# Output biases and column means of a cross-attention kernel by one product with a constant tile, under a new order of all engines

## What is computed

```
n_L0 = bv @ Wo          n_L1 = bv'_a @ Wo_a + bv'_v @ Wo_v   (bv' = ln2_b @ Wv + bv)
n_L3 = bv @ Wo          n_fc = ln_b @ fc_W
```

## Time and profile before

| | |
|---|---|
| three runs | 555.61, 556.83, 557.13 us |
| profiled execution, first to last instruction (span) | 557.1 us |
| busy: TensorE, VectorE, ScalarE, GpSimd | 98%, 86%, 80%, 86% of the span |
| mean granted clock of TensorE | 0.998 |
| transfers | 76.58 MB, mean 137 GB/s |

### The profile page before, as it was taken

The page is one execution under the profiler, slowest core; times in us unless marked ns, Lnnn a source line. Parts: engine busy times, 40 slices in busy tenths (PEclk is TensorE's granted clock), DMA queues, the critical chain, the costliest instruction groups (busy, mean ns, idle before and its releaser), DMA issues.

```text
span 557.1 us, 16210 instructions
## 1 busy us (share of the span) xinstructions
PE 545.8 (98%) x4492; PEld 534.9 (96%) x4492; DVE 478.4 (86%) x1472; ACT 447.2 (80%) x1568; POOL 480.7 (86%) x672
## 2 busy tenths in 40 slices
PE   8999999999999999999999999999999999999995
PEld 7999999999999999989999999999999999999994
DVE  2588799888999889989897997999898987998884
ACT  2799987889778797869879798877888979798663
POOL 4999997999988989979997899977999998766793
PEclk9999999999999999999999999999999999999999
DMA  8993472344553345453247263453433432221112
GB/s 238 352 326 126 118 215 90 121 147 149 172 168 111 113 143 152 149 174 124 80 139 202 67 190 102 145 172 122 139 122 115 124 105 78 77 96 58 39 40 95
DMA packets 74440, 76.58 MB, mean 137 GB/s; under 512 B 7664, under 2 KB 58224, under 8 KB 74352
## 3 DMA queue, kind: packets, MB, share of 16 engines
q1 hardware_dynamic: 74352, 75.55, 43.0%
HBM read 50.87 MB, written 24.64 MB: 136 GB/s over the span
## 4 chain that ended last, share of the span: by engine, by line
PE 87%; POOL 4%; DMA 3%; issue 2%; DVE 2%; SPq 1%; ACT 1%; DVEq 0%; POOLq 0%; ACTq 0%
PE bank L793 15%; PE bank L806 10%; PE bank L800 9%; PE bank L776 7%; PE bank L817 5%; PE bank L819 5%; PE bank L818 5%; PE bank L949 5%; PE bank L927 5%; PE bank L784 5%; PE bank L830 4%; PE bank L902 3%; PE bank L903 3%; PE bank L904 3%; DMA side_in<-in_side 1%
## 5 line engine op out<-in xcount | busy, mean ns | idle before, releaser
L1065 ACT ACTIVATE prob_L<-bank,neg_max_L 128x128 f32<-128x128 f32 x320 | 114.5, 375 | 15.7 <-DVE neg_max_L L1376 13.6
L1065 ACT ACTIVATION_READ_ACCUMULATOR prob_L<-bank,neg_max_L 128x1 f32 x320 | 68.3, 214 | 0.0
L1376 DVE TENSOR_REDUCE neg_max_L<-bank 128x2 f32<-128x256 f32 (+1 forms) x128 | 60.5, 479 | 7.1 <-PE bank L800 4.3
L1546 POOL TENSOR_TENSOR rstd_ln<-var_eps_ln,minus_half 128x2 f32<-128x2 f32 x64 | 45.2, 707 | 18.5 <-ACT var_eps_ln L1078 18.2
L994 ACT ACTIVATE oT_hi_L<-bank 128x256 fp32r<-128x256 f32 (+1 forms) x96 | 44.4, 471 | 12.4 <-PE bank L806 11.1
L1219 DVE TENSOR_TENSOR oT_lo_L<-bank,oT_hi_L 128x256 fp32r<-128x256 f32 (+1 forms) x96 | 47.2, 501 | 5.6 <-ACT oT_hi_L L994 4.9
L994 ACT ACTIVATE probT_L<-bank 128x256 f32<-128x256 f32 (+1 forms) x96 | 44.4, 470 | 9.0 <-PE bank L784 8.6
L1333 DVE BATCH_NORM_STATS2 stats_ln<-x 128x6 f32<-128x256 f32 x128 | 47.5, 413 | 0.2
L1219 DVE TENSOR_TENSOR xT_lo_L<-bank,xT_hi_L 128x512 fp32r<-128x512 f32 x64 | 43.1, 677 | 3.7 <-ACT xT_hi_L L994 3.5
L1611 POOL TENSOR_TENSOR x_bias<-x,bias_fc 128x512 f32<-128x512 f32 x32 | 41.1, 1285 | 5.8 <-DVE x L1409 5.8
L1588 POOL TENSOR_TENSOR xT_lo_L<-x_in,xT_hi_L 128x512 fp32r<-128x512 f32 x32 | 41.2, 1286 | 5.4 <-ACT xT_hi_L L994 5.4
(11 more groups left out here) (228 smaller groups left out, 2294.2 us busy)
## 6 DMA issues: line engine op xcount, KB each, us to landing
x_in<-in_x SPq DMA_DIRECT2D x32, 512.0 KB, 3.8
ctx_in<-in_ctx SPq DMA_DIRECT2D x32, 256.0 KB, 2.8
keys_out<-keys_turned SPq DMA_DIRECT2D x32, 256.0 KB, 2.2
keysT<-keys_out SPq DMA_DIRECT2D x128, 64.0 KB, 2.0
out<-y SPq DMA_DIRECT2D x32, 256.0 KB, 2.3
x_out<-x_turned SPq DMA_DIRECT2D x30, 256.0 KB, 2.2
x3T<-x_out SPq DMA_DIRECT2D x120, 64.0 KB, 2.3
side_in<-in_side SPq DMA_DIRECT2D x32, 128.0 KB, 2.7
```

The costliest lines, as they stand in the source:

```text
L1065: last = activation(at(prob[k], g)[:, b, :], block(bank, b), ACT.Exp, bias=at(neg_max[k], g)[:, b:b + 1], accum_out=at(total[k], g)[:, b:b ...
L1376: dve.tensor_reduce(at(neg_max[k], g)[:], scores, AX.X, ALU.max, negate=True).then_inc(done[f"max_{k}"], 1)
L1546: pool.tensor_tensor(at(rstd[k], g)[:], at(var_eps[k], g)[:], minus_half[:, 0:n], ALU.pow).then_inc(done[f"rstd_{k}"], 1)
```

## The change

The weighting moves from TensorE to VectorE. For an output bias, VectorE multiplies each row of the weight by its bias (the bias lies along the partitions, one column per half) and adds the halves: a `tensor_scalar`, then a `scalar_tensor_tensor` with both tensors in SBUF. For L1, L1v's two halves are added onto L1a's result. One product with `mean_of_D` then sums over the partitions, and `bias_plus` multiplies by 256 as it adds the row. For the column means VectorE adds the two halves first (`fc_added`, `M1_added`). `replicated` and its buffers are gone, and n_fc uses `output_bias` too. `load_vo_L3` waits for `weighted_L0` in place of `n_L0`. All other steps are as before.

```
@@ load_vo_L3 @@
                 prepared(sp, "N_L0")
-                prepared(sp, "n_L0")
+                prepared(sp, "weighted_L0")
...
@@ mean_M @@
-                    prepared(pe, f"M1_{a}")
+                    prepared(pe, f"M1_added_{a}")
                     bank = bank_for(pe, f"mean_M_{a}")
-                    for t in range(T):
-                        last = mm(bank[:, 0:P], mean_of_D[:], M1[a][:, t, :], start=t == 0, stop=t == T - 1)
-                    last.then_inc(done[f"mean_M_{a}"], 1)
+                    mm(bank[:, 0:P], mean_of_D[:], M1_added[a][:], start=True, stop=True).then_inc(done[f"mean_M_{a}"], 1)
...
-            def output_bias(key, attentions):
+            def output_bias(key, last_of):
+
                 def of():
+                    prepared(pe, "first_constant")
+                    prepared(pe, f"weighted_{last_of}")
                     bank = bank_for(pe, f"n_{key}")
-                    terms = []
-                    for a in attentions:
-                        prepared(pe, f"rep_{a}")
-                        pe.wait_ge(weights[f"{a}_vo"], TWO)
-                        terms += [(rep[a]["bv"][:, h, :], stage[a]["Wo"][:, h, :]) for h in range(T)]
-                    for n, (stationary, moving) in enumerate(terms):
-                        last = mm(bank[:, 0:D], stationary, moving, start=n == 0, stop=n == len(terms) - 1)
-                    last.then_inc(done[f"n_{key}"], 1)
+                    mm(bank[:, 0:D], mean_of_D[:], weighted[last_of][:], start=True, stop=True).then_inc(done[f"n_{key}"], 1)
                 return of
...
             def mean_fc():
-                prepared(pe, "gained_fc")
+                prepared(pe, "fc_added")
                 bank = bank_for(pe, "mean_fc")
-                for t in range(T):
-                    last = mm(bank[:, 0:D], mean_of_D[:], fc_gained[:, t, :], start=t == 0, stop=t == T - 1)
-                last.then_inc(done["mean_fc"], 1)
+                mm(bank[:, 0:D], mean_of_D[:], fc_added[:], start=True, stop=True).then_inc(done["mean_fc"], 1)
...
             def bias_plus(key, to, use, added):
-                dve.tensor_tensor(to[:], bank_of(use)[:, 0:D], added[:], ALU.add).then_inc(done[key], 1)
+                dve.scalar_tensor_tensor(out=to[:], in0=bank_of(use)[:, 0:D], scalar=float(D), in1=added[:],
+                                         op0=ALU.mult, op1=ALU.add).then_inc(done[key], 1)
...
+            def weighted_of(a):
+                def of():
+                    if a in LN_KEYS:
+                        prepared(dve, f"bvp_{a}")
+                        biases = [bvp[a][:, t, :] for t in range(T)]
+                    else:
+                        dve.wait_ge(weights["cols"], ONE)
+                        biases = [col("fc_b" if a == "fc" else f"{a}_bv", t) for t in range(T)]
...
+                    w = fcW if a == "fc" else stage[a]["Wo"]
+                    to = weighted[a]
+                    if a == "L3":
+                        prepared(dve, "n_L0")
+                    if a == "L1v":
+                        prepared(dve, "weighted_L1a")
+                        terms = range(T)
+                    else:
+                        before = smalls(1)
+                        dve.tensor_scalar(to[:], w[:, 0, :], biases[0], None, ALU.mult).then_inc(done["small"], 1)
+                        dve.wait_ge(done["small"], before + 1)
+                        terms = range(1, T)
+                    for t in terms:
+                        last = dve.scalar_tensor_tensor(out=to[:], in0=w[:, t, :], scalar=biases[t], in1=to[:],
+                                                        op0=ALU.mult, op1=ALU.add)
...
+            def M1_added_of(a):
+                    dve.tensor_tensor(M1_added[a][:], M1[a][:, 0, :], M1[a][:, 1, :], ALU.add).then_inc(done[f"M1_added_{a}"], 1)
...
+            def fc_added_of():
+                dve.tensor_tensor(fc_added[:], fc_gained[:, 0, :], fc_gained[:, 1, :], ALU.add).then_inc(done["fc_added"], 1)
...
-            def replicated(a):
...
-                    for t in range(T):
-                        of_bias = bvp[a][:, t, :] if a in LN_KEYS else col("fc_b" if a == "fc" else f"{a}_bv", t)
-                        last = pool.tensor_copy(rep[a]["bv"][:, t, :], of_bias.to_broadcast([P, P]))
```

More of the change, by code:

```diff
@@ L211 @@
-    "fetch_keys": [3843, 4466, 4975, 5800, 7201, 7659, 8977, 11642, 13747, 14340, 15211, 16940, 19159, 21191, 22040, 23608,
[11 rows of a table removed]
-}
-PREPARATIONS = {"run_up": 164, "M_L2": 534, "k_L2": 709, "N_L0": 1000, "n_L0": 912, "M_L0": 1364, "M_L1v": 1452, "m_L0": 1541, "m_L1v":
[14 rows of a table removed]
+    "load_x": [734, 1162, 1571, 2106, 2553, 2685, 3273, 4536, 5373, 6625, 7257, 9987, 11847, 11891, 12714, 16481, 17782, 19524, 19711,
[5 rows of a table added]
+    "load_ctx": [267, 1615, 1893, 2245, 2289, 2377, 2465, 2509, 2597, 2641, 9761, 11224, 12129, 14515, 15492, 18284, 20017, 21058, 22614,
[3 rows of a table added]
@@ new lines @@
+    "x_bias": [1589, 1714, 2112, 3012, 4160, 4408, 5846, 6197, 9605, 11605, 11729, 12582, 16015, 17153, 18238, 19450, 21290, 23407,
+        23967, 25608, 28368, 29872, 31709, 32162, 33287, 35031, 37666, 38725, 42421, 42669, 43881, 45634],
+    "stats_keys": [779, 2193, 2774, 3153, 4147, 4665, 5399, 6660, 7395, 8472, 10308, 13228, 14087, 15396, 15993, 18626, 21144, 22298,
+        23378, 24570, 27193, 28411, 29866, 30945, 33762, 35416, 36288, 37876, 39975, 41137, 43794, 44937],
+    "rstd_keys": [1016, 2775, 3523, 4670, 5137, 5361, 6321, 7014, 8404, 9954, 13249, 14935, 15159, 15780, 18761, 22629, 22894, 22993,
[15 rows of a table added]
@@ L245 @@
     "k_L2": [1],
-    "N_L0": [3],
-    "n_L0": [2],
-    "B2": [4, 7, 2, 5, 6, 0, 1, 3, 6, 7, 5, 5, 4, 7, 1, 3, 3, 3, 1, 7, 7, 4, 3, 4, 6, 3, 7, 7, 5, 3, 5, 4],
-    "M_L0": [5],
-    "M_L1v": [6],
-    "m_L0": [7],
-    "Q_L0": [0, 4, 3, 0, 6, 4, 0, 1, 5, 1, 1, 6, 0, 0, 5, 6, 6, 7, 7, 6, 5, 6, 2, 2, 0, 3, 3, 0, 0, 0, 3, 6],
-    "m_L1v": [1],
-    "S_L0": [5, 6, 5, 0, 1, 3, 1, 5, 3, 5, 5, 6, 6, 1, 0, 7, 4, 0, 3, 2, 3, 3, 1, 6, 3, 3, 3, 7, 5, 4, 4, 3],
-    "n_fc": [4],
+    "N_L0": [4],
+    "n_L0": [3],
+    "B2": [6, 2, 4, 7, 2, 6, 2, 2, 1, 7, 4, 1, 0, 4, 2, 2, 6, 5, 4, 1, 2, 7, 5, 1, 1, 4, 0, 6, 3, 2, 4, 4],
+    "M_L0": [2],
+    "M_L1v": [7],
+    "m_L0": [5],
+    "Q_L0": [1, 5, 4, 4, 1, 7, 6, 1, 3, 2, 0, 0, 4, 1, 3, 4, 6, 2, 2, 2, 0, 4, 5, 2, 2, 1, 5, 5, 1, 6, 5, 7],
+    "m_L1v": [2],
+    "S_L0": [5, 5, 2, 0, 1, 1, 1, 1, 2, 3, 4, 6, 3, 4, 2, 7, 7, 4, 5, 6, 1, 4, 1, 0, 2, 1, 7, 7, 4, 6, 4, 5],
+    "n_fc": [0],
     "mean_fc": [7],
[2 rows of a table removed]
[2 rows of a table added]
     "mean_M_L1v": [3],
[18 rows of a table removed]
-    "T_fc": [1, 5, 6, 5, 6, 6, 5, 1, 5, 6, 7, 3, 7, 4, 2, 7, 1, 5, 4, 5, 3, 3, 6, 2, 1, 3, 6, 5, 7, 7, 1, 5],
-    "OUT_fc": [1, 5, 6, 5, 5, 5, 0, 1, 5, 6, 1, 7, 7, 6, 4, 0, 2, 2, 0, 6, 2, 4, 3, 2, 1, 3, 6, 7, 3, 7, 3, 0],
[10 rows of a table removed]
[18 rows of a table added]
+    "T_fc": [1, 3, 3, 3, 4, 7, 2, 3, 2, 0, 5, 0, 4, 5, 2, 6, 0, 5, 1, 3, 2, 2, 0, 5, 4, 2, 7, 4, 2, 4, 5, 1],
+    "OUT_fc": [1, 1, 2, 3, 3, 7, 3, 3, 4, 6, 2, 0, 4, 7, 0, 5, 0, 3, 6, 3, 7, 6, 0, 4, 4, 6, 7, 4, 2, 6, 4, 6],
[9 rows of a table added]
 }
@@ L330 @@
                          + ["M0_L3", "gained_fc", "F_hi", "M_hi_L2", "Wv2_hi"]),
-             "VectorE": (["scaled"] + [f"M_lo_{a}" for a in ("L0", "L3")] + [f"N_lo_{a}" for a in ATTENTIONS] + [f"m_col_{a}" for a in ATTENTIONS]
-                         + [f"{w}_{a}" for w in ("wk_sum", "wv_sum", "bvp", "M_centred") for a in ("L1a", "L1v")]
+             "VectorE": (["scaled"] + [f"weighted_{a}" for a in ATTENTIONS + ["fc"]] + [f"M_lo_{a}" for a in ("L0", "L3")] + [f"N_lo_{a}" for a in ATTENTIONS] + [f"m_col_{a}" for a in ATTENTIONS]
+                         + ["fc_added"] + [f"{w}_{a}" for w in ("wk_sum", "wv_sum", "bvp", "M_centred", "M1_added") for a in ("L1a", "L1v")]
                          + ["bias_L0", "bias_L1", "bias_L3", "bias_fc", "centred_fc", "M_lo_L2", "k_bias2"]),
-             "GpSimd": (["first_constant", "constants", "rows_L1", "rows_L3", "F_lo", "Wv2_lo"] + [f"rep_{a}" for a in ATTENTIONS + ["fc"]]
+             "GpSimd": (["first_constant", "constants", "rows_L1", "rows_L3", "F_lo", "Wv2_lo"]
                         + [f"{w}_{a}" for w in ("wk_gained", "wv_gained", "M_lo") for a in ("L1a", "L1v")])}
@@ L437, in build @@
             inv_total[k] = ring(f"inv_total_{k}", [P, A[k] * GROUP])
-        stage, rep = {}, {}
+        stage, weighted = {}, {}
         with ExitStack() as staging:
@@ L453, in build @@
             bvp = {a: sb(f"bvp_{a}", [P, T, 1], where=staging) for a in ("L1a", "L1v")}
-            for a in ATTENTIONS + ["fc"]:
-                rep[a] = {"bv": sb(f"rep_bv_{a}", [P, T, P], where=staging)}
+            for a in ("L0", "L1a", "fc"):
+                weighted[a] = sb(f"weighted_{a}", [P, D], where=staging)
+            weighted["L1v"] = weighted["L1a"]
```

(16 more changed lines are left out.)

88 lines of the change are left out of this document (45 added, 43 removed), and 413 rows, old and new, of tables (PREPARATIONS, SEATS, STARTS).

## The result

The changed kernel takes 565.62 us (median of 4 runs, 564.62 to 566.85); beside them the kernel before took 556.98. The ratio is 1.016, interval 1.0133 to 1.0187: 8.6 us slower, where 3.7 us faster was forecast and nothing above 557 was in the range. A time is 1.8 us longer than the span of the same execution (566.31 and 564.5 in the profiled one).

A forecast was written before the change was run, and what follows sets the result against it. TensorE's queue was taken as the bound behind 13.76 us: 557.1 - 3.45 (products) + 0.5 (VectorE) + 0 (head) - 0.7 (order) + 0 (tail) = 553.45, less 0.3 for the median, 553.1 us; range 550 to 557.

The forecast's parts named there:

- Products removed: TensorE's preparation products: 18 of 4492 records gone, saving 3.45 us, bounds 3.0 to 3.9.
- rival 1: First 60 us: saved products become idle time while TensorE waits on GpSimd and transfers; 556.5 us, chance 0.17.
- Instructions added on VectorE: Weighing and adding: 13 instructions, 5.2 us, mostly covered by VectorE's idle time; charged 0.5 us, between 0 and 3.
- A wait between engines: VectorE instructions with two SBUF inputs wait for GpSimd, 0.6 us seen at 17.65; nine such instructions, cost left to rival 2.
- The head: New load order before the first groups: Q_L0 starts at 16.1 against 16.37; between -0.5 and +0.7 us, taken as 0.
- The new wait of load_vo_L3: In SP's queue, load_vo_L3 waits for weighted_L0 in place of n_L0; claimed to cost nothing.
- The rest of the order: From 60 to 530 us: fewer side loads behind stores; 0.7 us off, between 2.8 off and 3 added.
- Rival 3's slow side: New order doubles mid-kernel stalls and adds one microsecond in the tail: 557.6 us, chance 0.05.
- The base: Whole kernel: worked against the profiled span of 557.1 us, taking 0.3 off at the end for the median, 556.83.
- rival 2: VectorE and GpSimd block each other, nine waits of 0.6 us, to 60 us: 558.5 us, up to 561; chance 0.08.

The follow-up runs named there:

- e9: Kernel before, old order, with only four bias sums (L0, fc, L3, L1a) weighed on VectorE, running sum in PSUM: 559.01 us, ratio 1.0032.
- e11: Kernel before, old order, with only three bias sums (fc, L3, L1a) weighed on VectorE in PSUM: 557.44 us, ratio 1.0015.
- e13: Kernel before, old products kept, plus all 13 added VectorE instructions in SBUF, their sums unused by any product: 562.79 us, ratio 1.0104.
- e6: Changed kernel with the weighing's running sum in a PSUM bank instead of SBUF: 563.35 us, ratio 1.0112.
- e1: Changed kernel with the load of the columns again SyncE's first step: 565.60 us, ratio 1.0157.
- e5: Changed kernel's new order with the old products and GpSimd copies, columns loaded first: 561.76 us, ratio 1.0087.
- e3: Changed kernel's new order with the old products and GpSimd copies of the kernel before: 560.85 us, ratio 1.0073.
- e12: e9 plus six constant filler products ahead of M_L0, where TensorE waited for WkT_L: 558.65 us, ratio 1.0020.

## Why the prediction was wrong, point by point

**Products removed** (3.45 us): right in number, 4474 instructions, and in size where a row shows it (the one product left of mean_fc runs from 19.87 to the next start at 20.31, 0.44 us). The sentence built on it, "one microsecond of product less is one microsecond less of time, wherever it is removed behind 13.76", failed. e9 and e11 remove 1.7 and 1.3 us and get none of it. Their traces show the shorter queue waiting for transfers and ScalarE up to 21 us. That was rival 1, at 0.17. Both also put 8 and 6 instructions on VectorE, and no run takes products away without that, so how much those cost is not shown.

**Instructions added on VectorE** is the step that failed most. Sized at 5.2 us and charged 0.5, since idle time "covers the sum"; they took 12.0 in the changed kernel, and in e13, where no product waits for their results, the same 13 cost 5.6 us. The rows of the nearest shape all read one operand from PSUM, and that was just what made them 0.42: in e6, with PSUM, they take 0.42 to 0.49 again. Half of VectorE's idle time up to 60 us, 10.5 of 21.3 us, stood before 13.76, before most of its data had landed; from 20 to 40 it had 4.66 us, and in the changed kernel 0.38.

**A wait between engines**: the right mechanism, seen at 17.65, and put at 0.08. I counted nine instructions; two of the four tensor_scalar took 1.42 and 1.43 us as well. I bounded the case at 561, because I took the wait at its own length. The runs show three more terms: what stands behind it in VectorE's queue, TensorE's wait for it, and half the clock after that wait. "Four or more of the nine run before 20, where VectorE is half idle": four do, but VectorE is half idle there only in the kernel before; with them it works 5.38 of the 6.24 us.

**The head**: Q_L0 at 17.46, forecast 16.1, within the 15 to 18 that I had set as its test. I followed x 0 and fcW through the new queue of loads and left out cols, on which k_L2 waits 1.94 us. That miss cost nothing in itself (e1, e5): with the columns first Q_L0 starts at 18.18. I had also left out that n_L0, ahead of Q_L0, waits for a weighted_L0 that stands behind the statistics (1.05 us), the products at half rate up to 16 us, and the 2.44 us that the two instructions on fcW took, priced at 0.84. The new wait of load_vo_L3, at "nothing", was issued at 14.65 for 12.83, since N_L0 ran late; what that cost was not isolated.

**The rest of the order** (−0.7): wrong sign. e3 puts the new order and its banks at +4.3 us with nothing else changed. In its profiled execution 2 products of the loss stand before 60 us and 13 behind; the mean over all kernels puts 3.3 us behind 60. Rival 3's slow side, 557.6 at 0.05, was nearer. I read idle time in the profile (2.79 us) as what an order could win or lose there. After the change it is 0.55, and yet less work is done. What in the order makes the distances between products longer was not found.

**The base**: the profiled execution of before had a span of 557.1, and so, by the 1.8 us of the other runs, a time near 558.9. I set the span against the median of times and took off 0.3; by that reckoning it was about 2 us slower than the median.

Together, for the two profiled executions: 5.1 us net up to 60 us, where the 3.45 saved have been used up by the collisions, the waits behind them and the clock, and 1.6 us from there to 530, 6.7 of 7.4. With the mean of all kernels, 3.3, for the steady part it would be 8.4 of the 8.6 between the medians; that this pair owes 3.3 to it is an estimate, since its own counts say 1.6 beside a slow execution of before. Two of my signs came true at once, rival 1's (TensorE's idle time from 13.76 to 60 went from 0.27 to 4.37 us) and rival 2's (0.9 us an added instruction); I had priced each alone.

## What to carry to other kernels

Before work is moved from TensorE to VectorE, look at where its operands lie and at what GpSimd does at that minute: price an instruction with its tensors in SBUF at GpSimd's longest instruction (1.4 us here), unless one side can stand in PSUM (0.5 us here). Count the products begun by a given time, since busy and idle time hide slow products and short pauses. In a head that is tight against loads, as here, a product saved is a longer wait unless something else is ready, and that wait can cost the clock as well.

## What the runs showed of the hardware that I had not expected

- A tensor_scalar of 128x256 from SBUF to SBUF, with a single tensor input, took 0.32 to 1.43 us beside GpSimd; with its result in PSUM 0.45 to 0.49 in e6, a little more than the shortest and none of them long. In e13 even one of 128x2 took 1.27 us beside an instruction of GpSimd of 1.25; the same one took 0.25 before.
- The pair at 35.01 stayed out for two of GpSimd's instructions, and these took 1.40 and 1.44 us in place of 1.28: both sides pay. Over the whole kernel GpSimd is busy 480.3 us in the changed kernel and 478.4 in e6, with the same steps on it.
- The granted clock of a profile is shown as 1.00 in the first stretch of e9 and of before, while products of 256 columns follow each other there by 0.21 us, and later, at full rate, by 0.12 (e12, from 16.39 on). In e1 it is shown as 1.00 from 14 to 20 us, with products 0.21 us apart up to 16.75. The distance between products is the surer reading in the head.
- One pause of 2.24 us in a busy stretch was followed by 3 us at a granted clock of 0.50.
